# Channel 0 subtracted from all channels, and the Fourier sum moved to ScalarE and GpSimd, in a two-layer metaformer kernel

## The reference, cut to what matters

```
# layer 0
x = x + deform_conv(ln_c(x), w_off, w_conv)        # 3x3 taps, offsets from a 3x3 conv
t = tokens(x)                                      # one token per pixel, 128 channels
p = top2(softmax(ln_t(t) @ router_w + router_b)), renormalised
t = t + sum_e p_e * (ln_t(t) @ expert_w[e] + expert_b[e])     # 8 experts
# layer 1
x = x + real(ifft2(mix(fft2(ln_c(x)), alphas, betas)))
t = t + soft MoE(ln_t(t))                          # per image, 64 experts, top 8 tokens of each
```

## Time and profile before

| | |
|---|---|
| time, median of 3 runs | 3882.41 us (3878.23 to 3882.8) |
| the profiled execution, time | 3885.28 us |
| the profiled execution, span | 3883.5 us |
| busy: TensorE / VectorE / ScalarE / GpSimd | 94% / 76% / 40% / 38% of the span |
| granted TensorE clock, mean | 0.956 of full speed |
| DMA | 709.87 MB, mean 183 GB/s |

### The profile page before, as it was taken

The page is one execution under the profiler, slowest core; times in us unless marked ns, Lnnn a source line. Parts: engine busy times, 40 slices in busy tenths (PEclk is TensorE's granted clock), DMA queues, the critical chain, the costliest instruction groups (busy, mean ns, idle before and its releaser), DMA issues. The chain is left out here.

```text
span 3883.5 us, 89684 instructions
## 1 busy us (share of the span) xinstructions
PE 3661.0 (94%) x31447; PEld 2461.6 (63%) x31447; DVE 2944.5 (76%) x9683; ACT 1568.3 (40%) x4561; POOL 1473.4 (38%) x2661
## 2 busy tenths in 40 slices
PE   5999999999999999999979999999999999996567
PEld 4777777777777777777745666666666666654345
DVE  4666666666666666666648999999999999996534
ACT  3444444444444444444411434344334434444124
POOL 4444444444444444544412333333333333333210
PEclk7999999999999999999979999999999999998755
DMA  5655555555555554555527777777777777884689
GB/s 106 108 95 106 103 94 97 97 105 106 90 99 96 107 104 94 96 97 96 88 82 264 272 275 275 268 273 276 274 270 270 277 275 269 282 311 162 249 311 392
DMA packets 611682, 709.87 MB, mean 183 GB/s; under 512 B 62257, under 2 KB 494257, under 8 KB 594849
## 3 DMA queue, kind: packets, MB, share of 16 engines
q1 hardware_dynamic: 505760, 630.17, 58.2%
q10 hardware_dynamic: 104448, 71.85, 5.9%
q0 software_dynamic: 1024, 2.10, 0.2%
HBM read 521.20 MB, written 181.63 MB: 181 GB/s over the span
## 5 line engine op out<-in xcount | busy, mean ns | idle before, releaser
L423 PE MATMUL a_sb<-a_sr,wcv 128*128 128x512 f32 (+3 forms) x2820 | 1052.2, 515 | 0.8 <-DVE a_xo L551 0.8
L405 PEld LDWEIGHTS a_sb<-a_tt,a_win 32*128 32x128 f32 x19008 | 646.5, 186 | 120.8 <-issue 120.1
L423 PEld LDWEIGHTS a_sb<-a_sr,wcv 128*128 128x128 f32 x2820 | 492.8, 190 | 334.2 <-issue 289.2
L405 PE MATMUL a_sb<-a_tt,a_win 32*128 32x144 f32 x19008 | 678.9, 295 | 22.4 <-DMA a_win<-xtp 9.0
L1171 DVE TENSOR_TENSOR b_P<-b_P,b_x 128x1024 f32<-128x1024 f32 x512 | 619.8, 1212 | 0.0
L509 DVE COPY a_sr<-a_sb 128x432 f32<-128x432 f32 (+14 forms) x1172 | 419.2, 412 | 208.6 <-PE a_sb L405 208.6
L482 ACT COPY a_sr<-a_sb 128x432 f32<-128x432 f32 (+14 forms) x1172 | 362.9, 389 | 360.8 <-PE a_sb L405 360.8
L1074 PE MATMUL b_z<-b_P,b_ew 128*128 128x512 f32 x1024 | 463.3, 595 | 0.0
L1077 PE MATMUL b_z<-b_P,b_ew 128*128 128x512 f32 x1024 | 460.3, 592 | 0.0
L1300 POOL TENSOR_TENSOR b_ss<-b_st 128x12 f32<-128x12 f32 (+2 forms) x139 | 30.0, 216 | 1049.7 <-DVE b_pp L1245 963.0
L545 DVE STREAM_TRANSPOSE a_tt<-a_sx 128x576 f32<-128x576 f32 x520 | 398.4, 767 | 14.2 <-POOL a_sx L576 5.4
(11 more groups left out here) (184 smaller groups left out, 5343.2 us busy)
## 6 DMA issues: line engine op xcount, KB each, us to landing
b_P<-pd SPq DMA_DIRECT2D x128, 2048.0 KB, 7.8
a_win<-xtp SPq DMA_DIRECT2D x2144, 36.0 KB
a_xin<-in_x SPq DMA_DIRECT2D x128, 256.0 KB, 6.0
xtp<-a_tn ACTq DMA_DIRECT2D x128, 256.0 KB, 2.3
x1d<-a_xo SPq DMA_DIRECT2D x128, 256.0 KB, 5.7
b_x<-x1d SPq DMA_DIRECT2D x128, 256.0 KB, 7.7
x2d<-b_xa SPq DMA_DIRECT2D x128, 256.0 KB, 3.5
pw<-x3d SPq DMA_DIRECT2D x128, 256.0 KB
```

Source lines behind the costliest of these rows:

```text
L405: t = e.matmul(d[:, 0:3 * m_, :, NU_ * i:NU_ * i + NU_], win[32 * q:32 * q + 32, half_of(Q, j) % NWH, NWIN // 3 * h + i, :], m, start=(j = ...
L423: t = e.matmul(ob[:, r:r + m, :], k["wcv"][:, 3 * (2 - kr) + kx, :], rows[:, :, t_, :], start=(t_ == 0 and r == 0), stop=(t_ == 8))
```

## The change

Channel 0 of x1 is subtracted from all channels of a pixel. Then row 0 of the expert products is free: with x1's channel 0 set to 1 and row 0 of `P` filled with the plain weights, row 0 of the expert weights carries the biases, and the ninth product goes. The parts:

- Setup: `wcv` gets a semaphore of its own, and VectorE subtracts the first output column from the other 127.
- First phase: SyncE loads channel 0 of x, 4 rows, to partitions 1 to 127 of a new tile `xz` (`load0`), and GpSimd subtracts it from x (`level`) before VectorE adds the convolution.
- Second phase, start: SyncE loads the biases over row 0 of the centred expert weights, VectorE subtracts 1 from one column of it (for the sum with x1), and TensorE waits for both.
- `read` has 137 columns; the last one brings the true channel 0. `lr` has 8 buffers.
- `level` (SyncE): ones from SBUF over row 0 of x1, one transfer a group. `spread` is two transfers: the plain weights to partition 0, the scaled ones to partitions 1 to 127. `spread_b`, `pb` and the ninth product go.
- ScalarE copies `T2` to `xa` in four instructions with the true channel 0 as bias.
- `x3`: ScalarE scales `ZC` in four instructions, GpSimd adds x2 in one (128 x 512), and VectorE keeps the statistics, as a stage of its own one step later. `store3`, `norm3`, `turn3`, `gate`, `best`, `sums` and `collect` move one step later, and there is one step more.

```diff
 # setup_phase, VectorE
+            e.wait_ge(wcv_in, 16)
+            e.tensor_tensor(k["wcv"][:, :, 1:128], k["wcv"][:, :, 1:128],
+                            k["wcv"][:, :, 0:1].to_broadcast([128, 9, 127]), ALU.subtract).then_inc(centred, 1)
 # order_a
+        if 0 <= s - 1 < NG:
+            put(t0 + 6, "load0", s - 1)
         if 0 <= s - 2 < NG:
+            put(t0 + 4, "level", s - 2)
 # phase_a, VectorE, residual
+                w.wait_ge(levelled, G + 1)
 # phase_a, GpSimd
+            elif o[0] == "level":
+                G = o[1]
+                w.wait_ge(filled, 1)
+                w.wait_ge(x0_in[G % 2], 16 * (G // 2 + 1))
+                w.wait_ge(convolved, 2 * G + 2)
+                e.tensor_tensor(xin[:, G % NX, :], xin[:, G % NX, :], xz[:, G % 2, :], ALU.subtract
+                                ).then_inc(levelled, 1)
 # phase_a, SyncE
+            elif o[0] == "load0":
+                G = o[1]
+                b, q = divmod(G, GI)
+                w.wait_ge(levelled, G - 1)
+                e.dma_start(xz[1:128, G % 2, :],
+                            ins["x"][b * 128, 4 * q * W:4 * q * W + 512].partition_broadcast(127)
+                            ).then_inc(x0_in[G % 2], 16)
 # phase_bc, TensorE
+        w.wait_ge(weights_ready, 2)
...
-                    t = e.matmul(RD[:, r // 2, r % 2, 0:136], x1[:, G % NX1, r, :], iw[:, :], start=True, stop=True)
+                    t = e.matmul(RD[:, r // 2, r % 2, 0:137], x1[:, G % NX1, r, :], iw[:, :], start=True, stop=True)
...
-                    e.matmul(ZE[u][:, :, :], ew[:, x, :], P[:, G % NPB, :, x, :], start=False, stop=False)
-                w.wait_ge(pb_in[G % NPC], 16 * (G // NPC + 1))
-                e.matmul(ZE[u][:, :, :], ebm[:, :], pb[:, G % NPC, :], start=False, stop=True).then_inc(mixed, 1)
+                    t = e.matmul(ZE[u][:, :, :], ew[:, x, :], P[:, G % NPB, :, x, :], start=False, stop=(x == 7))
+                t.then_inc(mixed, 1)
...
-                w.wait_ge(x3_ready, G)
+                w.wait_ge(x3_scaled, G)
 # phase_bc, ScalarE
-                e.copy(xa[:, G % 3], T2[:, :, :]).then_inc(xa_ready, 1)
+                w.wait_ge(lr_ready, G + 1)
+                for r in range(4):
+                    t = e.activation(xa[:, G % 3, r, :], T2[:, r, :], ACT.Identity, bias=lr[:, G % NLR, r, 8:9])
+                t.then_inc(xa_ready, 1)
+            elif stage == "x3":
...
+                for r in range(4):
+                    t = e.activation(x3t[:, G % 3, r, :], ZC[:, r, :], ACT.Copy, scale=rsr[:, G, 3 - r:4 - r])
+                t.then_inc(x3_scaled, 1)
 # phase_bc, VectorE
-            w.wait_ge(P_in[G % NPB], 16 * (G // NPB + 1))
+            w.wait_ge(P_in[G % NPB], 32 * (G // NPB + 1))
+            w.wait_ge(x1_in[G % NX1], 32 * (G // NX1) + 32)
...
-            elif stage == "x3":
+            elif stage == "stats3":
+                w.wait_ge(x3_ready, G + 1)
+                w.wait_ge(scaled, G + LAG)
 # phase_bc, GpSimd
+            elif stage == "x3":
+                w.wait_ge(x2_in[G % 3], 16 * moves(G))
+                w.wait_ge(x3_scaled, G + 1)
+                e.tensor_tensor(x3t[:, G % 3], x3t[:, G % 3], x2r[:, G % 3], ALU.add).then_inc(x3_ready, 1)
 # phase_bc, SyncE
+        w.wait_ge(centred, 5)
+        e.dma_start(ew[0:1, :, :], ins["eb"][:, :, :]).then_inc(eb_in, 16)
...
-                e.dma_start(P[:, G % NPB].rearrange("p r e x -> p (r e x)"),
+                e.dma_start(P[0:1, G % NPB].rearrange("p r e x -> p (r e x)"),
+                            pd[G % NPT * 64:G % NPT * 64 + 32, :].rearrange("a x -> (a x)").partition_broadcast(1)
+                            ).then_inc(P_in[G % NPB], 16)
+                e.dma_start(P[1:128, G % NPB].rearrange("p r e x -> p (r e x)"),
                             pd[G % NPT * 64 + 32:G % NPT * 64 + 64, :].rearrange("a x -> (a x)"
-                                                                                 ).partition_broadcast(128)
+                                                                                 ).partition_broadcast(127)
                             ).then_inc(P_in[G % NPB], 16)
-            elif stage == "spread_b":
...
+            elif stage == "level":
+                w.wait_ge(read, G + 1)
+                e.dma_start(x1[0:1, G % NX1], k["ones"][0:1, None, :].to_broadcast([1, 4, 128])
+                            ).then_inc(x1_in[G % NX1], 16)
```

More of the change, by code:

```diff
@@ L48, in setup_phase @@
     sem = lambda n: ctx.enter_context(nc.semaphore("s_" + n))
-    filled, loaded, w_in, summed, centred = (
-        sem(n) for n in ("filled", "loaded", "w_in", "summed", "centred"))
+    filled, loaded, w_in, summed, centred, wcv_in = (
+        sem(n) for n in ("filled", "loaded", "w_in", "summed", "centred", "wcv_in"))
     T = ctx.enter_context(nc.psum_tensor("s_t", [128, 162], F32))
@@ L284, in phase_a @@
         sem(n) for n in ("rs_step", "z_step", "oc_ready", "hats_ready", "weighed_pool"))
+    levelled = sem("levelled")
     x_in = [sem(f"x_in{i}") for i in range(NX)]
+    x0_in = [sem(f"x0_in{i}") for i in range(2)]
     tn_out = [sem(f"tn_out{i}") for i in range(NTN)]
@@ L900 @@
 NU = 10
[L901 to L907, removed]
+NX1, NPB, NPT, NLR = 9, 3, 4, 8
+STEP = (("load", -3), ("load2", LAG - 2), ("read", 0), ("level", 1), ("turn2", 6), ("fourier", LAG), ("turn3", LAG + 3),
+        ("store2", 6), ("turn_p", 2), ("experts", 4), ("p_out", 2), ("scales", 1), ("best", LAG + 4), ("mixed", 5),
+        ("stats1", 0), ("stats2", 6), ("stats3", LAG + 1), ("x3", LAG), ("store3", LAG + 1), ("spread", 2),
+        ("norm3", LAG + 2), ("gate", LAG + 3), ("experts2", 4), ("place", 5), ("sums", LAG + 4), ("weights", 1),
+        ("turn_scale", 7), ("collect", LAG + 5))
+NS = NG + LAG + 1
 NCH, EC, NW, AHEAD = 8, 8, 8, 3
@@ L938, in order_b @@
     out = [("load", G) for G in range(3)]
-    for s in range(NG + LAG + 5):
+    for s in range(NG + LAG + 6):
         for stage, lag in STEP:
@@ L1024, in phase_bc @@
     P_in = [sem(f"P_in{i}") for i in range(NPB)]
-    pb_in = [sem(f"pb_in{i}") for i in range(NPC)]
     x2_out = [sem(f"x2_out{i}") for i in range(3)]
@@ L1187, in vector @@
         w.wait_ge(r_step, 1)
+        e.memset(iw[0:1, 128:136], 0.0).then_inc(weights_ready, 1)
+        w.wait_ge(eb_in, 16)
+        e.tensor_scalar(ew[0:1, :, 0:1], ew[0:1, :, 0:1], -1.0, None, ALU.add).then_inc(weights_ready, 1)
         for stage, G in order:
@@ L1258, in vector @@
                 t.then_inc(stats2, 1)
[L1259 to L1273 removed]
+            elif stage == "stats3":
+                w.wait_ge(x3_ready, G + 1)
+                w.wait_ge(scaled, G + LAG)
+                for r in range(4):
+                    t = e.bn_stats(st[:, (G + LAG + 1) % 2, 8 + r, :], x3t[:, G % 3, r, :])
                 t.then_inc(stats3, 1)
```

96 lines of the change are left out of this document (46 added, 50 removed).

## The result

The changed kernel takes 13,661.35 us, median of 4 runs (13,656.07 to 13,676.11), beside 3,880.96 us for the kernel before in 4 runs on the same chip: a ratio of 3.520, 95% interval 3.515 to 3.524. The profiled execution took 13,664.4 us, its span is 13,662.8. It is slower, as forecast, and 1% above the forecast of 13,525.

The account below looks back on a forecast made before the run. TensorE was taken to bound both phases, with DMAs hidden; one DMA engine would bound the changed kernel: 3885.3 + 9060 (second phase) + 555 (first phase) + 25 (starts and ends) = 13,525 us, range 12,700 to 14,700.

Parts of the forecast that it names:

- The number of engines: Both phases' 127-row transfers: engines are the largest number up to 16 dividing the rows, so 127 gets one.
- The price of a spread: Second phase: 2.081 MB on one engine at 26.6 GB/s takes 78.2 us, plus 2.1 us fixed.
- rivals 3 and 4: Second phase's spread price: (3) 94.2 us, total 15,515 us, chance 0.05; (4) 72.5 us, total 12,230 us, chance 0.08.
- The wait for the small store: Second phase: next spread waits for the weights' store, queued behind the spread: 1.9 us, plus 0.45 issue; period 83 us.
- The first phase: First phase: one engine's packets, TensorE pauses and 1 us for its clock give 19.4 us a group, +555 us.
- window term: First phase: window loads' share on the broadcast's engine, 2.9 to 9.4 us a group.
- rival 2: First phase: clock falls throughout, phase +1890 us in place of +555, total 14,860 us; chance 0.10.
- Starts and ends: Phase edges: one step more 11.8 us, two fixed costs 4.2, drain partly at low clock; together 25 us.
- What compute was said to need: Second phase, per step: TensorE 10.93 us, VectorE about 10.4; only 50 us could come out, if DMAs stay hidden.
- Rival 1: Second phase: 127 rows shared over many engines, spread near 7.8 us, total 3850 us; chance 0.05.
- GpSimd's add is free: Second phase: GpSimd, busy 62 of 200 us, takes the 128x512 add; nearest row 1.18 us.
- The loop's 11.4 us: Second phase: VectorE's weights 7.17 us, GpSimd's scales 4.14, signal 0.1; limits the step to 11.4 us.

Follow-up runs that it names:

- e4: Kernel before the change with only its spread of 128 rows cut into 5 and 123 rows: 6492.07 us.
- e5: Kernel before the change with only its spread of 128 rows cut into 1 and 127 rows: 13,105.96 us.
- e3: Changed kernel with only the spread cut into 112 and 15 rows, and `level` five slots later in GpSimd's order: 4663.9 us.
- e10: Changed kernel with only the spread cut into 112 and 15 rows, and `load0` five slots earlier in SyncE's order: 4710.96 us.
- e1: Changed kernel with both transfers of 127 rows, spread and `load0` broadcast, cut into 112 and 15 rows: 4192.49 us, ratio 1.080.
- e6: From e1: spread is one transfer of 128 rows again, partition 0's plain weights follow in a later one-row transfer: 3976.74 us, ratio 1.024.
- e7: From e6: Fourier sum back on VectorE in four instructions, ScalarE's scaling and GpSimd's add gone: 3866.26 us, ratio 0.996.
- e8: From e6: GpSimd's scales wait for the weights and products of one group earlier, Fourier sum stays on GpSimd: 3862.41 us, ratio 0.995.
- e11: From e8: GpSimd's 128x512 add in the Fourier sum made in four pieces of 128x128: 3844.19 us, ratio 0.990.

## Why the prediction was right, and where it was not

**The number of engines** (step one of the DMA part): right. 127 rows went to one engine, at a share of 0.06; e4 shows the same rule at 123 rows and three engines (a share of 0.19), and e5 shows it in the kernel before, where nothing else was changed.

**The price of a spread**: right. Predicted were 78.2 us of transfer and 2.1 fixed; from the issue at 5013.65 to VectorE's first product at 5094.56 are 80.9. The price of 26.6 GB/s an engine, taken from a stretch in which all 16 were busy, holds for an engine alone, and rivals 3 and 4 fall with it (periods of 98.7 and 77).

**The wait for the small store**: right, and the size too. From VectorE's first product at 5094.56 to the next spread at 5097.22 are 2.7 us, and the sum had 1.9 + 0.45. Period 83.43 against 83, +9115 against +9060. The terms add to 82.65; the rounding up to 83 is worth 44 us and made the forecast better by chance. The reason given was a queue behind the spread; in fact SyncE is also held in its issues. Both come from the one engine, and the runs don't separate them.

**The first phase**: +583 against +555, 19.61 us a group against 19.4. The sum had a window term of 2.9 to 9.4 us, of which the middle was taken, so the agreement is in part luck: e3 and e10 show that 0.8 and 0.4 us a group hang on the places of `level` and `load0`, which the sum did not have. The pauses of 3 to 4 us and the 1 us for the clock came out as said: from 97 to 1000 us TensorE is busy 742.21 of 903 us at a clock of 0.92, that is 16.1 us of work a group (15.0 before) and 3.5 of idling. The clock was not at 0.50 throughout, so rival 2 falls.

**The term that was mis-sized** is "Starts and ends", 25 us. Measured are 78.5 + 4.2 - 1 = 82. There are 127 intervals but 128 spreads: the last one's landing, some 81 us against the 7.8 of the earlier trace rows, lies behind the last interval and was counted nowhere. That alone is 73 us. The total came out 139 us (1.0%) low: 55 in the second phase, 28 in the first, 57 here.

**What compute was said to need** had no say in the result, and was wrong. Rival 1, shared rows, gave 3850 us; e1 is that case and took 4192, and e6, with the rows in one transfer, 3977. The forecast that GpSimd's add is free because GpSimd has 62 of 200 us busy looked at its busy share, not at what it does to VectorE. While the loop was closed, the move of the Fourier sum made a step 0.75 us longer than leaving it on VectorE (e6 against e7, 12.30 and 11.55); once the loop was open it took 0.9 us of VectorE's time in waits. The loop's 11.4 us, read from the kernel before, left out the 1.1 us that the add puts into it, and became 12.3. VectorE's "about 10.4" is 11.2 in e8 (0.982 x 11.44).

## What to carry to other kernels

Before a row is split off a transfer, factor the rows that are left: by these runs 128 rows, or 112 and 15, are shared widely, 123 have three engines and 127 one, and one such transfer holds up what the same engine issues behind it, small ones too. If one partition must differ, send all 128 and write the one afterwards (e6 against the changed kernel: 3977 against 13,661 us). Work moved to an idle GpSimd was not free where VectorE's instructions met it: look at the duration of VectorE's small instructions before and after. Cutting the moved instruction into pieces gave back a little here (e11 against e8, 18 us).

## What was not expected of the hardware

SyncE's issue of a transfer, 0.2 to 0.6 us when its queue is short, lasts far longer while one engine works off 127 rows of 16 KB, although the other 15 engines mostly idle: the load right behind the spread (L1370) has a median of 34.5 us and a longest of 46.0. SyncE is then not only waiting for data; its timeline has nothing else in that time.

A spread cut in 112 and 15 rows kept the DMA engines busy for 92% of the time at 229 GB/s; one of 128 rows brings 259 to 277 GB/s at 73 to 78%. The cause is open.

The turns between the two engines work against GpSimd as well. In the timeline of e11, GpSimd instructions of 128x12 that meet a product of VectorE last over a microsecond, and their neighbours a fifth of that:

```profile
2804.97 1.22 DVE L1219 TENSOR_TENSOR b_P<-b_P,b_x 128x1024 f32<-128x1024 f32 x1
2805.19 1.06 POOL L1349 TENSOR_SCALAR b_ss<-b_ss 128x12 f32<-128x12 f32 x1
...
2806.34 0.21 POOL L1351 TENSOR_TENSOR b_ss<-b_ss 128x12 f32<-128x12 f32 x1
```
